# Routing by index table: each expert tile gathers its own token rows, instead of rows scattered into a zeroed buffer

## The reference, cut to what matters

```python
scores = softmax(xf @ w_gate)                 # 1024 tokens, 8 experts
weights, idx = top_k(scores, 2)               # each token goes to 2 experts
exp_x[flat_e, pos] = xf[tok]                  # rows sorted by expert (capacity 2048, never reached)
h = einsum('ecd,edf->ecf', exp_x, c_fc)       # 512 -> 1536, per expert
a, g = split(h, 2); h = silu(a) * g
exp_out = einsum('ecf,efd->ecd', h, c_proj)   # 768 -> 512
out = sum over the 2 choices of exp_out[flat_e, pos] * weight
```

## Time and profile before

| | us |
|---|---|
| median of 3 runs (2139.08 to 2141.41) | 2140.75 |
| the profiled execution, its own time | 2137.46 |
| its span in the trace | 2135.7 |
| PE busy in the span | 1910.4 (89%) |
| DVE / ACT / POOL busy | 1345.1 / 1137.0 / 124.1 |
| mean granted TensorE clock | 0.935 of full speed |

### The profile page before, as it was taken

How to read it: one execution, slowest core, us unless ns; L and a number is a source line. 1 busy time by engine, 2 the same in 40 slices (tenths; PEclk the granted TensorE clock), 3 DMA queues, 4 the chain that set the end, 5 groups by cost and what they waited for, 6 DMA issues and landing times. The chain is left out here.

```text
span 2135.7 us, 31829 instructions
## 1 busy us (share of the span) xinstructions
PE 1910.4 (89%) x10570; PEld 1511.8 (71%) x10570; DVE 1345.1 (63%) x2457; ACT 1137.0 (53%) x1878; POOL 124.1 (6%) x153
## 2 busy tenths in 40 slices
PE   7978875599999589999999999999977999888998
PEld 4647764599999467787878787878755676665654
DVE  4755663599999364545353636363527899986676
ACT  5753331588888254444453535454435666656654
POOL 0000001200000111000000000000000000001221
PEclk9998985799999799999999999999998788879999
DMA  7410004244431521100000000000204000020000
GB/s 259 158 55 1 0 0 202 87 175 152 187 142 54 202 75 60 35 30 34 29 34 29 34 29 34 29 34 29 79 28 147 1 1 1 1 84 1 0 20 20
DMA packets 25897, 137.47 MB, mean 64 GB/s; under 512 B 4066, under 2 KB 4194, under 8 KB 22116
## 3 DMA queue, kind: packets, MB, share of 16 engines
q1 hardware_dynamic: 19588, 116.18, 14.7%
q0 software_dynamic: 6240, 20.45, 2.8%
HBM read 116.17 MB, written 20.45 MB: 64 GB/s over the span
## 5 line engine op out<-in xcount | busy, mean ns | idle before, releaser
L109 PE MATMUL PS<-cT,qs 128*128 128x512 f32 x1152 | 295.5, 402 | 9.0 <-ACT pb L1406 7.0
L109 PE MATMUL PS<-pT,cN 128*128 128x512 f32 x1152 | 270.2, 392 | 1.7 <-DVE pT L1501 1.7
L109 PEld LDWEIGHTS PS<-cT,qs 128*128 128x128 f32 x1152 | 209.4, 189 | 59.8 <-issue 15.1
L109 PEld LDWEIGHTS PS<-pT,cN 128*128 128x128 f32 x1152 | 213.9, 188 | 45.5 <-DVE pT L1501 1.9
L109 PE MATMUL PS<-fw,xgT 128*128 128x384 f32 x1104 | 204.2, 340 | 3.1 <-DVE xgT L1049 3.0
L109 PEld LDWEIGHTS PS<-fw,xgT 128*128 128x128 f32 x1104 | 191.5, 189 | 8.4 <-issue 4.5
L1049 DVE TENSOR_TENSOR fw<-W,fw 128x1536 fp32r<-128x1536 f32 x92 | 159.3, 1753 | 44.7 <-ACT fw L972 44.7
L1496 DVE TENSOR_REDUCE nmax<-PS 128x1 f32<-128x512 f32 x128 | 87.7, 685 | 157.0 <-PE PS L109 156.9
L109 PE MATMUL PS<-ws,xT 128*128 128x512 f32 x672 | 180.6, 427 | 6.6 <-DVE ws L563 4.9
L109 PEld LDWEIGHTS PS<-ws,xT 128*128 128x128 f32 x672 | 137.6, 207 | 46.1 <-issue 11.3
L972 ACT ACTIVATE fw<-W 128x1536 fp32r x92 | 134.2, 1486 | 50.2 <-issue 50.2
(11 more groups left out here) (259 smaller groups left out, 3390.6 us busy)
## 6 DMA issues: line engine op xcount, KB each, us to landing
W<-in_fc SPq DMA_DIRECT2D x8, 3072.0 KB, 10.5
cT<-in_ctxT SPq DMA_DIRECT2D x16, 768.0 KB, 5.4
raw_pj<-in_proj SPq DMA_DIRECT2D x8, 1536.0 KB, 6.5
ct_in<-in_ctxT SPq DMA_DIRECT2D x16, 768.0 KB
cn_in<-in_ctxN SPq DMA_DIRECT2D x16, 768.0 KB
W<-in_w SPq DMA_DIRECT2D x2, 4096.0 KB, 12.9
routed_x<-zero SPq DMA_DIRECT2D x23, 256.0 KB, 5.4
xg<-routed_x POOLq DMA_DIRECT2D x23, 256.0 KB, 3.2
```

The lines of the kernel that those rows point to most:

```text
L109: mm = nc.tensor.matmul(out, lhs(m, s), rhs(n, s), start=(opens and (s, m, n) == terms[0]), stop=((s, m, n) == terms[-1]))
```

## The change

It does four things.

1. The zero fill of `routed_x` is gone, with its buffer, its memset and its 23 DMAs. In its place SP stores the normalised tokens `xn` in token order to a DRAM buffer `normal_x`: 8 plain DMAs of 256 KB in the routing block, each behind its tile's normalisation, put between the load of expert 0's `fc` weights and that of its `proj` weights.
2. A table `index[row, tile]` of the token that each slot holds is computed in the routing block. For each pair DVE splits the slot into tile number and row (`tidf`, `modf`), builds one-hot matrices of the row (`at_row`, 16 of 128 x 128) and of the tile times the token number (`token`, 16 of 128 x 24), and PE sums their 16 products. Slots that no pair holds get token 0.
3. The owners and their parity are computed later, between DVE's last one-hot matrix and its copy of the product. The slots' integer copies come last.
4. In the main block each tile's load is an indirect gather from `normal_x` by the table's column. The gather of tile 0 is issued in the routing block. In POOL's loop the store that follows the gather of s is that of s-3 instead of s-2, so each gather stands one tile earlier against the stores.

```diff
 # cosine_layer, SyncE and GpSimd
-                sp.wait_ge(s_zero, BASE + 1)
-                PER = ET // (NT - 1)
                 with sp.Fori(0, NT - 1) as i:
                     for u in range(2):
                         sp.wait_ge(c_lo, BASE + 2 * i + u + 1)
                         sp.dma_start(cT[:, u], a["ctxT"][2 * i + 2 + u]).then_inc(s_ct[u], 16)
-                    for n in range(PER):
-                        sp.dma_start(xg_d[bass.ds((PER * i + n) * P, P), :], zero[:, :]).then_inc(s_xg0, 16)
-                for n in range(PER * (NT - 1), ET):
-                    sp.dma_start(xg_d[n * P:(n + 1) * P, :], zero[:, :]).then_inc(s_xg0, 16)
-                sp.wait_ge(s_xg0, BASE + 16 * ET)
...
-                nc.gpsimd.memset(zero[:, :], 0.0).then_inc(s_zero, 1)
 # expert_layer
+        def gather(s):
+            nc.gpsimd.indirect_dma_start(
+                out=xg[:, s % 2, :], out_offset=None, in_=xn_d,
+                in_offset=bass.IndirectOffsetOnAxis(index[:, s:s + 1], axis=0)).then_inc(xg_in[s % 2], 16)
...
                     sp.dma_start(gate[:, :, :], a["gate"]).then_inc(s_gate, 16)
-                    load(sp, 0)
-                    load(sp, 1)
+                    sp.dma_start(rowid[:, :], a["consts"][:, CN_ROW:CN_END]).then_inc(s_row, 16)
+                    sp.dma_start(raw_fc[:, 0], a["fc"][0]).then_inc(s_fc, 16)
+                    for t in range(NT):
+                        sp.wait_ge(s_norm, BASE + t + 1)
+                        sp.dma_start(xn_d[t * P:(t + 1) * P, :], xn[:, t, :]).then_inc(s_xn, 16)
+                    sp.dma_start(raw_pj[:, 0], a["proj"][0]).then_inc(s_pj, 16)
+                    sp.wait_ge(s_fc, BASE + 16)
+                    sp.dma_start(raw_fc[:, 1], a["fc"][1]).then_inc(s_fc, 16)
+                    sp.wait_ge(s_pj, BASE + 16)
+                    sp.dma_start(raw_pj[:, 1], a["proj"][1]).then_inc(s_pj, 16)
...
-                    pool.wait_ge(s_norm, BASE + NT)
-                    pool.wait_ge(e.s_xg0, BASE + 16 * ET)
-                    pool.wait_ge(s_slot, BASE + 2)
-                    for t in range(NT):
-                        for c in range(2):
-                            nc.gpsimd.indirect_dma_start(
-                                out=xg_d, out_offset=bass.IndirectOffsetOnAxis(slot[:, t, c:c + 1], axis=0),
-                                in_=xn[:, t, :], in_offset=None).then_inc(s_scat, 16)
-                    pool.wait_ge(s_scat, 16 * 2 * NT)
+                    pool.wait_ge(s_xn, BASE + 16 * NT)
+                    pool.wait_ge(s_index, BASE + 1)
+                    gather(0)
...
+                    pe.wait_ge(s_token, BASE + 2)
+                    for n in range(2 * NT):
+                        if n % 4 == 0:
+                            pe.wait_ge(s_at, BASE + n // 4 + 1)
+                        mm = nc.tensor.matmul(ps[3][:, 0:ET + 1], at_row[:, n, :], token[:, n, :],
+                                              start=(n == 0), stop=(n == 2 * NT - 1))
+                    mm.then_inc(i_mm, 1)
...
 # VectorE, behind starts; place, pick and slotf stand first now, with both choices in slotf
+                    ch.link(nc.vector.tensor_scalar(tidf[:, :, :], slotf[:, :, :], 1.0 / P, (P - 1) / 2.0 / P,
+                                                    ALU.mult, ALU.subtract))
+                    ch.link(nc.vector.tensor_scalar(tidf[:, :, :], tidf[:, :, :], ROUND, ROUND, ALU.add, ALU.subtract))
+                    ch.link(nc.vector.scalar_tensor_tensor(modf[:, :, :], tidf[:, :, :], -float(P), slotf[:, :, :],
+                                                           ALU.mult, ALU.add))
+                    ve.wait_ge(s_row, BASE + 16)
+                    TS = [P, NT, ET + 1]
+                    tile_no = rowid[:, P + NT:P + NT + ET + 1]
+                    for c in range(2):
+                        ch.link(nc.vector.tensor_tensor(in_tile[:, :, :], tile_no.unsqueeze(1).to_broadcast(TS),
+                                                        wide(tidf[:, c, :], TS), ALU.is_equal))
+                        nc.vector.tensor_tensor(token[:, c * NT:(c + 1) * NT, :], in_tile[:, :, :],
+                                                wide(rowid[:, P:P + NT], TS), ALU.mult).then_inc(s_token, 1)
+                        if c == 0:
+                            ve.wait_ge(s_token, BASE + 1)
+                    for q in range(4):
+                        c, t0 = divmod(4 * q, NT)
+                        AT = [P, 4, P]
+                        nc.vector.tensor_tensor(at_row[:, 4 * q:4 * q + 4, :],
+                                                rowid[:, 0:P].unsqueeze(1).to_broadcast(AT),
+                                                wide(modf[:, c, t0:t0 + 4], AT), ALU.is_equal).then_inc(s_at, 1)
 # then under, ownf, owner, edge, halff, parity as before, and
+                    ve.wait_ge(i_mm, BASE + 1)
+                    nc.vector.tensor_copy(index[:, :], ps[3][:, 0:ET + 1]).then_inc(s_index, 1)
+                    for c in range(2):
+                        nc.vector.tensor_copy(slot[:, :, c], slotf[:, c, :]).then_inc(s_slot, 1)
...
 # main block, GpSimd
-                for s in range(ET):
+                for s in range(1, ET):
                     if s >= 2:
                         pool.wait_ge(x_mm, BASE + s - 1)
-                    nc.gpsimd.dma_start(xg[:, s % 2, :], xg_d[s * P:(s + 1) * P, :]).then_inc(xg_in[s % 2], 16)
-                    if s >= 2:
-                        store(s - 2)
-                store(ET - 2)
-                store(ET - 1)
+                    gather(s)
+                    if s >= 3:
+                        store(s - 3)
+                for s in range(ET - 3, ET):
+                    store(s)
```

More of the change, by code:

```diff
@@ L49 @@
 CN_ALL = CN_PICK + 9 * P + 8
+CN_ROW = CN_ALL
+CN_TOKEN = CN_ROW + P
+CN_TNO = CN_TOKEN + NT
+CN_END = CN_TNO + ET + 1
 def constant_table():
-    t = np.zeros((P, CN_ALL), np.float32)
+    t = np.zeros((P, CN_END), np.float32)
     p = np.arange(P)
@@ L70, in constant_table @@
     t[:, CN_PICK + 9 * P:CN_ALL] = p[:, None] % 8 == np.arange(8)[None, :]
+    t[:, CN_ROW:CN_ROW + P] = p[None, :]
+    t[:, CN_TOKEN:CN_TOKEN + NT] = np.arange(NT)[None, :] * P + p[:, None]
+    t[:, CN_TNO:CN_END] = np.arange(ET + 1)[None, :]
     return t
@@ L196, in cosine_layer @@
         xT = sbuf("xT1", [P, DK, P])
-        zero = sbuf("zero1", [P, D])
         ln = Norm(nc, e, "1", sbuf, ps[7], xT)
@@ L207, in cosine_layer @@
         s_w0, s_x2 = sem("s_w0_1"), sem("s_x2_1")
-        s_zero = sem("s_zero1")
         dve = sem("dve1")
@@ L704, in expert_layer @@
             total, tiles, ends, starts = (rbuf(n, [P, NE]) for n in ("total3", "tiles3", "ends3", "starts3"))
-            slotf = rbuf("slotf3", [P, NT])
+            slotf, tidf, modf = (rbuf(n, [P, 2, NT]) for n in ("slotf3", "tidf3", "modf3"))
+            rowid = rbuf("rowid3", [P, CN_END - CN_ROW])
+            at_row = rbuf("at_row3", [P, 2 * NT, P], F32R)
+            in_tile, token = rbuf("in_tile3", [P, NT, ET + 1]), rbuf("token3", [P, 2 * NT, ET + 1], F32R)
             under = rbuf("under3", [1, ET, NE])
             ownf, halff = rbuf("ownf3", [1, ET]), rbuf("halff3", [1, ET])
-            s_gate, g_mm = sem("s_gate3"), sem("g_mm3")
+            s_gate, g_mm, s_row, s_xn = sem("s_gate3"), sem("g_mm3"), sem("s_row3"), sem("s_xn3")
+            s_token, s_at, i_mm = sem("s_token3"), sem("s_at3"), sem("i_mm3")
             s_var, s_rstd, s_norm, s_turn, s_xT = sem("s_var3"), sem("s_rstd3"), sem("s_norm3"), sem("s_turn3"), sem("s_xT3")
@@ L829, in _ @@
                     ch.link(nc.vector.tensor_tensor(
+                        place[:, :, :], ps[2][:, 0:NT * NE].rearrange("p (t e) -> p t e", t=NT),
+                        starts[:, :].unsqueeze(1).to_broadcast(TE), ALU.add))
+                    for c in range(2):
+                        ch.link(nc.vector.tensor_tensor(pick[:, :, :], place[:, :, :], oh[c][:, :, :], ALU.mult))
+                        ch.link(nc.vector.tensor_reduce(slotf[:, c, :], pick[:, :, :], AX.X, ALU.add))
+                    ch.link(nc.vector.tensor_scalar(tidf[:, :, :], slotf[:, :, :], 1.0 / P, (P - 1) / 2.0 / P,
[19 more added lines that the diff above has]
+                                                wide(modf[:, c, t0:t0 + 4], AT), ALU.is_equal).then_inc(s_at, 1)
+                    ch.link(nc.vector.tensor_tensor(
                         under[:, :, :], ends[0:1, :].unsqueeze(1).to_broadcast([1, ET, NE]),
@@ L835, in _ @@
                     nc.vector.tensor_copy(edge[:, :], ends[0:1, :])
[L837 to L840, removed]
-                        ch.link(nc.vector.tensor_tensor(pick[:, :, :], place[:, :, :], oh[c][:, :, :], ALU.mult))
-                        ch.link(nc.vector.tensor_reduce(slotf[:, :], pick[:, :, :], AX.X, ALU.add))
-                        nc.vector.tensor_copy(slot[:, :, c], slotf[:, :]).then_inc(s_slot, 1)
```

(9 more changed lines are left out.)

21 lines of the change are left out of this document (7 added, 14 removed).

## The result

The kernel after takes 2131.6 us (median of 7 runs, 2128.84 to 2135.16) against 2140.75. The ratio is 0.9961 with an interval of [0.9947, 0.9974]: faster by 9 us, where I had forecast 17.6 and a range that ended at 2128.5. The runs were made in rounds, each with its own executions of before, and the rounds of the experiments on chips of their own. Before's mean is 2140.3 us beside this result and 2141.4, 2143.5 and 2140.6 (standard errors 0.6 to 1.0) in the three rounds of the experiments, 52 runs with a mean of 2141.9. So I compare a kernel with before of its own round. After was run in two of them: 8.4 us faster here, 9.0 in a later one, together **8.8 us, +- 0.8** (one standard error, as in all that follows; 13 runs of after, mean 2131.8). Against the 52 runs it would be 10.1. The profiled execution of after took 2128.84 us, the quickest of its seven, with a span of 2127.0.

What follows compares the result with a forecast made beforehand. PE was taken to bound the main loop, with an uncovered 28 us idle stretch before it. The routing chain's shortening gave 17.6 us, all other terms zero: 2140.75 - 17.6 = 2123.15 us, range 2119.5 to 2128.5.

Steps and rivals of the forecast that it cites:

- DVE to the table: Routing block, from `place` to the first `at_row`: 1.25, 0.6, 1.5 and 0.7 us of DVE operations, ending at 366.65 us.
- PE's 16 products: Routing block, PE's sum of the table: 3.4 us at half clock, 0.21 each like the gate's, ending at 370.4 us.
- Owners beside the products: Routing block: 1.7 us of small DVE operations, hidden beside PE's products.
- POOL's gather: Routing block: the gather starts 1.0 us after its last input, issues from 371.65 to 372.85 us and lands at 375.15.
- The end of the block: Routing block: 0.1 us of DRAIN for one DMA and 0.2 for the branch, at 373.15; ACT's split at 374.9.
- The start of the main block: From ACT's first split the weight chain takes 4.07 us, so PE starts at 379.0 instead of 396.60 us.
- Stores of `xn`, zero fill: Added stores cost zero, up to 5 us without cover; removing the fill gains 0, its rival 2.0 us more (8%).
- The loop: Main loop: zero change; gathers have 20.9 us before use, against a landing of 5.1 at most.
- The rule on DVE: Main loop, slower rival (3%): making gather descriptors holds DVE; 2149.6 us at 2.2 us lost per gather. Rows showed no hold.
- the carry from the chain to the median: Whole kernel: the chain's 17.6 us taken off the median of the runs, 2140.75, giving 2123.15 us.
- the clock at the start of the main block: Start of the main block: up to 1.8 us lost or won if TensorE's clock rises at another moment.
- the DRAIN rival: End of the routing block: DRAIN waits for the gather in flight, POOL done at 375.3; gain 15.4, kernel 2125.4 us; 17%.

Runs made afterwards that it cites:

- 31 pads in after: The changed kernel plus 31 VectorE copies of a 128 x 512 tile, result unused, between expert layer and the attention's loop; ratio to before 0.9998.
- kernels with equal pads: Before and after, each with the same number of unused VectorE tile copies after the expert layer: after faster by 15.1 us with four, 16.9 with 31.

## Why the prediction was wrong

**The sign and the mechanism of the gain were right.** The chain was priced nearly to the tenth up to the table.

- *DVE to the table.* Forecast 1.25 + 0.6 + 1.5 + 0.7; measured from `place` 1.29, 0.62, 1.54, and PE's first product at 366.28 (366.65 forecast).
- *PE's 16 products.* 3.56 us against 3.4: the half clock's price of the gate's products was the right row.
- *Owners beside the products.* Hidden, DVE even waited 0.37 us for PE; 1.5 us if put ahead (forecast 1.7).
- *POOL's gather.* 370.92 and 1.16 long (371.65 and 1.2). It started 0.86 us after the copy, between my bounds. All times of the chain stand 0.5 us earlier than in the sum, since the layer begins 0.5 us earlier in this profile.
- *The end of the block.* **This is the first step that failed**: "I charge 0.1 for one, and 0.2 for the branch ahead of it". The DRAIN took 3.94 us and ended at 374.6, instead of 373.15; counted from `starts` it ended 2.0 us late. The charge for each DMA was not wrong: with everything landed the DRAIN of the main block takes 3.98 us behind 48 DMAs and 3.91 behind after's 47. What the step put at nothing is the wait before it: the DRAIN first waits until POOL's DMA in flight has landed and ends 0.08 us behind it, 3.94 us with the gather and 0.034 without. My rival on it had the mechanism and the right landing (forecast end 375.3), and at 15.4 the right size for the chain, 15.3. I had given it 17%, and its 2125.4 for the kernel missed as well, for the second step below.
- *The start of the main block.* From DRAIN's end to ACT's split 2.1 us (1.76), then 4.04 us to PE (4.07). PE at 380.78 instead of 379.0, and 2.3 us late counted from `starts`: 17.6 less 2.3 is the 15.3 measured.
- *Stores of `xn`, zero fill.* Nothing, as priced. SP had issued all by 351.6 and POOL did not wait for it.
- *The loop.* The sum was right at zero and the reason partly wrong. "A landing of 5.1 at most" was read in a layer whose loads are small; beside the 3 MB loads it is 12.1. It stays under the lead of 20.9, and it is above 7.3. The edit that I had costed at nothing, one tile of lead, is worth 36 us (27.3 slower than before, where after is 8.8 faster), and 42.9 in the loop itself.
- *The rule on DVE.* With 22 gathers in the loop DVE's split lasts 1755 ns, 1753 before: nothing is held. But POOL is. The making of a gather's descriptors takes 0.95 us beside DVE operations that read one input from PSUM, and 1.66 to 2.01 us where it starts beside a split of the `fc` weights, which has both inputs in SBUF, in all 19 gathers from 409 us on. POOL's and DVE's timelines of after:

```profile
392.39 0.95 POOL L679 DMA_INDIRECT xg<-normal_x,index  x1 [14.30 <-PE PS L947]
...
422.86 1.87 POOL L679 DMA_INDIRECT xg<-normal_x,index  x1 [0.30 <-issue]
```

```profile
392.78 0.69 DVE L1080 TENSOR_TENSOR xgT<-PS,xgT 128x512 fp32r<-128x512 f32 x1
...
420.45 3.42 DVE L1080 TENSOR_TENSOR fw<-W,fw 128x1536 fp32r<-128x1536 f32 x2
```

In the kernel with a lead of one tile six gathers met an idle DVE, and took 0.98 to 0.99. In all 19 what is added to 0.955 us is the time that the two run together, less 0.09 to 0.10. The Trainium skill (GPSIMD Engine Reference, Key points) names GpSimd beside DVE with two SBUF inputs as contending. The rows agree for this split and show that here POOL alone pays. But they don't bear the rule out for every such pair: the `pw` split that follows within the same gathers has both inputs in SBUF too and runs beside them for 0.36 to 0.69 us at no cost, and beside the `qs` splits of the earlier trace rows, 0.55 us with both inputs in SBUF, five gathers took 0.95 to 0.99. What sets the first pair apart is open. No run was made for it alone, so it stands on these rows.

**The second failed step, and the larger one, is the carry from the chain to the median.** The sum took a gain of 17.6 in one stretch over to the median of the runs, with "up to 1.8 us" for the clock at the start of the main block alone. The chain has 15.2 (means of three profiles) and the runs 8.8, so 6.4 us are lost on the way: 0.9 at the loop's end, where the row shows a lower clock; 0.3 in cross-attention; and some 5 that lie in no fixed place. The profiles have 2.3 before the gate and 0.7 in the last layer, neither outside their own scatter.

In the runs the loss goes with the clock. Over 52 runs of before the time falls by 1.5 us for each 0.001 of mean granted clock (correlation -0.94, a rest of 1.1 us), and by 1.5 to 1.7 within each round. The removed 15 us ran at half clock; taking them out should lift the mean by 15.3 x (0.932 - 0.50) / 2130 = 0.0031. It didn't: in the round that has the clocks of both, the means are 0.9326 for before (11 runs) and 0.9323 for after (6). An estimate from these: 0.0034 too little is worth 5.2 us, and 15.2 - 5.2 = 10.0, against 9.0 +- 1.0 measured there.

**What stays open is why.** The later layers of the three repeated profiles of before are no quicker than after's, so their place in time did not make those layers quick. But the table above shows a loss of 2.4 to 5.2 us in all four kernels that stand 13.7 us or more earlier, and about none with 31 pads in after, where the later stages stand where before's do. So neither place in time nor the code of the change is excluded. A cost of the changed code alone is the less likely: it would be there with pads too, and between kernels with equal pads the gain is whole. No run singles a cause out.

The range ended at 2128.5 because the DRAIN rival stood in it alone, and because the runs' own spread was taken from three runs that lay 2.3 us apart; the seven beside the result lie 7.4 apart. With the DRAIN and the scatter of the clock in layers that the change doesn't touch it would have ended near 2133.

## What to carry to other kernels

Before an early issue is put ahead of a barrier, ask whether the engine's end of block waits for it: if it does, everybody waits for the landing, and behind the barrier the same DMA may be hidden. Price a landing from a row with the same neighbours on the DMA queues: here the gathers beside a 3 MB load took 11.5 us and more, all others less than 5. And when a profile is one of several executions with a scatter of their own, cut it into stages, profile before more than once, compare runs with before of the same round, and give each gain the width of the stages that nobody touched.

## What was not expected of the hardware

- POOL's DRAIN with a gather in flight ends 0.08 us behind the gather's landing, in nine traces of nine (3.94 us long in after); in the same block without the gather it takes 0.034. With all DMAs landed it still takes 1.37 us behind 16, 3.91 behind 47 and 3.98 behind 48; other work of POOL counts as well, for it takes 1.37 in the feed-forward block of after, which has 33 vector operations of POOL and no DMA.
- A gather of 128 rows (256 KB) beside a 3 MB load of SP lands in 11.5 to 12.1 us in after, otherwise in 3.2 to 4.8.
- An indirect DMA's descriptors take POOL 0.95 us, and up to 2.01 beside VectorE's split of the `fc` weights, whose own time doesn't change; two other splits with both inputs in SBUF don't hold it.
- Identical executions of before spread over 12 us on one chip (2135.7 to 2147.9) and go with the mean granted clock; in one stretch of 177 us the same 1280 matmuls keep PE busy for 140.4 to 147.6 us.
- Lengthening a stage by 2.8 us did not make the kernel slower (10.6 +- 1.3 us under before, where after is 8.8 +- 0.8), nor did 1.5 us more of routing (11.7 +- 0.8): an edit of this size can't be read from the total here, only from the stage.
